# A graph layer on one core: block 0 from whole f32 inputs, gathers one step later, a reordered beginning

## The reference

```python
r = edge_vec / norm(edge_vec);  sh1 = sqrt(3) * r
s1 = concat(x[src][:, :8], x[dst][:, :8]);  v1 = the same of the vectors
w  = relu(emb @ fc1_w1 / sqrt(10)) @ fc1_w2 / 4          # 512 weights of an edge
s_t, v_t = sums over u of s1, v1 . sh1, s1 * sh1, v1 with w   # 8 scalars, 8 vectors
w2 = relu(emb @ fc2_w1 / sqrt(10)) @ fc2_w2 / 4          # 384 weights
scal, gates, vecs = the same kind of sums of s_t, v_t with w2
edge_out = concat(tanh(scal), vecs * tanh(gates)) * edge_weight
x = layernorm(x + segment_sum(edge_out, dst))
```

## Time and profile before

| | us |
|---|---|
| median of 3 runs | 746.08 (746.05 to 746.92) |
| the profiled execution | 744.64 |
| its span (first to last instruction) | 742.8 |
| PE busy | 687.2 (93%) |
| DVE busy | 691.7 (93%) |
| ACT busy | 560.2 (75%) |
| POOL busy | 528.0 (71%) |
| mean granted TensorE clock | 0.97 |

### The profile page before, as it was taken

One profiled execution on the slowest core, in us unless ns is written; L12 is line 12 of the kernel. 1 busy time (PEld: TensorE's weight loads), 2 busy tenths in 40 slices (PEclk: granted clock), 3 DMA queues, 4 the chain that ended last, 5 costly groups with the idle time before them and its releaser, 6 DMA issues.

```text
span 742.8 us, 19328 instructions
## 1 busy us (share of the span) xinstructions
PE 687.2 (93%) x5990; PEld 282.9 (38%) x5990; DVE 691.7 (93%) x1231; ACT 560.2 (75%) x1281; POOL 528.0 (71%) x653
## 2 busy tenths in 40 slices
PE   2359999999999999999999999999999999999984
PEld 2113334434443444344344444334434443444321
DVE  7488999999999999999999999999999999999986
ACT  3238887887888778888888888877788888878752
POOL 5676888778876887688768886787778876887200
PEclk7569999999999999999999999999999999999998
DMA  5412211111111211121112111211121111111000
GB/s 132 112 34 47 47 32 28 40 46 28 30 42 27 50 26 42 28 47 31 43 26 45 29 43 27 48 31 27 40 46 29 28 39 26 41 27 27 20 1 23
DMA packets 45822, 28.49 MB, mean 38 GB/s; under 512 B 23299, under 2 KB 43941, under 8 KB 45721
## 3 DMA queue, kind: packets, MB, share of 16 engines
q1 hardware_dynamic: 31402, 19.43, 9.9%
q0 software_dynamic: 13312, 6.84, 6.0%
q10 hardware_dynamic: 1006, 0.96, 0.5%
HBM read 22.46 MB, written 4.74 MB: 37 GB/s over the span
## 4 chain that ended last, share of the span: by engine, by line
PE 87%; DVE 4%; issue 2%; ACT 1%; POOL 1%; DVEq 0%; ACTq 0%
PE ps L1073 16%; PE ps L986 14%; PE ps L1004 13%; PE ps L993 9%; PE ps L1053 8%; PE ps L974 6%; PE ps L1029 5%; PE ps L1066 4%; PE ps L1060 3%; PE ps L964 3%; PE ps L1041 3%; PE ps L948 2%; PE ps L1021 2%; DVE p_s L751 2%; ACT v_s L528 1%
## 5 line engine op out<-in xcount | busy, mean ns | idle before, releaser
L374 POOL DMA_INDIRECT xs<-in_xp,src_i x416 | 401.0, 964 | 115.2 <-issue 104.3
L751 DVE TENSOR_TENSOR p_s<-ps,h 128x2048 f32<-128x2048 f32 x104 | 238.3, 2292 | 21.6 <-PE ps L1073 20.9
L791 DVE TENSOR_TENSOR z_s<-ps,h 128x2048 f32<-128x2048 f32 x104 | 237.6, 2284 | 1.3 <-PE ps L1029 1.2
L528 ACT CAST v_s<-ps 128x512 bf16<-128x512 f32 x312 | 182.2, 584 | 48.3 <-PE ps L986 43.2
L1073 PE MATMUL ps<-f,w_f 32*128 32x512 f32 x832 | 119.7, 642 | 4.3
L986 PE MATMUL ps<-p_s,sum_m 128*32 128x512 f32 x832 | 111.7, 605 | 0.6 <-DVE p_s L751 0.5
L1004 PE MATMUL ps<-z_s,w_z 128*32 128x512 f32 x832 | 110.8, 605 | 1.5 <-DVE z_s L791 1.5
L494 ACT COPY f<-ps 128x512 f32<-128x512 f32 x104 | 61.0, 587 | 41.9 <-PE ps L974 41.5
L993 PE MATMUL ps<-v_s,less 128*128 128x512 bf16 x208 | 81.1, 390 | 2.8 <-ACT v_s L528 2.6
L416 POOL TENSOR_TENSOR along<-fe,r 128x192 f32<-128x192 f32 x104 | 54.2, 521 | 32.8 <-ACT fe L506 26.3
L1053 PEld LDWEIGHTS ps<-ident,u 128*128 128x128 f32 x416 | 43.8, 141 | 87.6 <-issue 87.0
(11 more groups left out here) (129 smaller groups left out, 848.7 us busy)
## 6 DMA issues: line engine op xcount, KB each, us to landing
emb<-e_dram SPq DMA_DIRECT2D x309, 30.0 KB
xs<-in_xp,src_i POOLq DMA_INDIRECT x416
e_dram<-e_part SPq DMA_DIRECT2D x7, 360.0 KB, 3.0
e_in<-in_emb SPq DMA_DIRECT2D x8, 240.0 KB, 2.9
window<-x_dram SPq DMA_DIRECT2D x104, 7.9 KB
eo_all<-in_vec_t SPq DMA_DIRECT2D x1, 528.0 KB, 5.0
x_dram<-eo_all SPq DMA_DIRECT2D x1, 525.0 KB
place<-place_dram SPq DMA_DIRECT2D x26, 20.0 KB
```

The costliest lines, as they stand in the source:

```text
L374: nc.gpsimd.indirect_dma_start(xs_r[n][:, t, :], None, xp, bass.IndirectOffsetOnAxis(src_i[:, m * T + t:m * T + t + 1], axis=0)).then_inc( ...
L528: nc.scalar.copy(v_s[:], v_ps).then_inc(v_step, 1)
L751: nc.vector.tensor_tensor(p_s[:], ps[:, 0:4, :], h1_r[m % 2][:].unsqueeze(1).to_broadcast([128, 4, BE]), ALU.mult).then_inc(p_done, 1)
L791: nc.vector.tensor_tensor(z_s[:], ps[:, 0:4, :], h2_r[k % 3][:].unsqueeze(1).to_broadcast([128, 4, BE]), ALU.mult).then_inc(z_done, 1)
```

## The change

- The first block (WHOLE = 1) takes its MLP inputs and weights in f32, in whole, from the arguments (e_whole, w_whole), so its hidden layers need no parts; the buffers emb serve blocks 1 on.
- SP: bases and w2a are loaded earlier, the register loads for the first three windows are done ahead, windows 0 to 2 go out together, then the store of the first group of MLP inputs (which was in ScalarE's list), window 3, and the rest in another order. ScalarE's list loses the store, the wait for it and block 0's three loads; it gains the load of the rest of the vectors.
- POOL: clears the sums acc at the start (VectorE did), gathers blocks 0 and 1 whole before the steps, no longer makes the first group's remainders, and gathers block i + 4 in step i instead of i + 5.
- VectorE: constants that were made after the directions stand ahead of the first remainder of x; the first remainder of x stands ahead of the places; the first group's remainders are made here; the weights of the hidden layers are split in step -2, the repeat matrices made in step 0, the rest of the directions spread over steps -2 and 1 to 3; the sums are not cleared here.
- TensorE: hidden_1 of block 0 in step -3, two idle matmuls (keep_warm) at the end of step -2, waits for constants split accordingly.

```diff
+WHOLE = 1
...
+        e_whole = early(32 + HID, WHOLE * BE).rearrange("p (b e) -> p b e", b=WHOLE)
+        w_whole = early(32 + HID, 128)
...
-                base = sp.value_load(bases[0:1, m:m + 1], min_val=0, max_val=N - 1)
+                    base = sp.value_load(bases[0:1, m:m + 1], min_val=0, max_val=N - 1)
+                else:
+                    base = first_bases[m]
...
+            sp.dma_start(bases[:], bases_row).then_inc(bases_loaded, 16)
+            sp.dma_start(w2a_s, w2a).then_inc(w2a_loaded, 16)
+            for n in range(2):
+                sp.dma_start(e_whole[32 * n:32 * n + HID], emb[0:WHOLE * HID].rearrange("(b h) e -> h b e", h=HID)
+                             ).then_inc(whole_loaded, 16)
+                sp.dma_start(w_whole[32 * n:32 * n + HID], w1[0:HID, n, :]).then_inc(whole_loaded, 16)
             load_super(0)
-            sp.dma_start(w1_s, w1).then_inc(weights_loaded, 16)
-            sp.dma_start(w2a_s, w2a).then_inc(weights_loaded, 16)
-            sp.dma_start(bases[:], bases_row).then_inc(bases_loaded, 16)
+            sp.dma_start(w1_s, w1).then_inc(w1_loaded, 16)
...
+            sp.wait_ge(bases_loaded, 16)
+            first_bases = [sp.value_load(bases[0:1, m:m + 1], min_val=0, max_val=N - 1) for m in range(3)]
...
             load_window(1)
+            load_window(2)
+            store_super(0)
+            load_window(3)
             sp.wait_ge(emb_zeroed, 1)
-            load_window(2)
             load_emb(1)
-            sp.dma_start(vt[:, TA:TILES, :], vec_t[:, TA:TILES, :]).then_inc(vect_rest_loaded, 16)
-            load_window(3)
-            sp.dma_start(src_i[:, TA:TILES], src_t[:, TA:TILES]).then_inc(src_loaded, 16)
-            load_emb(2)
             sp.wait_ge(place_stored, 32)
             load_places(1)
-            sp.dma_start(w_z[:].rearrange("p n c -> p (n c)"), w2b).then_inc(weights_loaded, 16)
+            load_emb(2)
+            sp.dma_start(w_z[:].rearrange("p n c -> p (n c)"), w2b).then_inc(w2b_loaded, 16)
+            sp.dma_start(src_i[:, TA:TILES], src_t[:, TA:TILES]).then_inc(src_loaded, 16)
+            load_places(2)
             sp.dma_start(wgt_s[:], wgt).then_inc(wgt_loaded, 16)
             sp.dma_start(dst_i[:], dst_t).then_inc(dst_loaded, 16)
...
+            nc.gpsimd.memset(acc[:], 0.0).then_inc(acc_zeroed, 1)
             pool.wait_ge(src_loaded, 16)
-            gather(0, 0, 3)
-            rest_of_emb(0, 0)
-            gather(0, 3, T)
+            gather(0, 0, T)
+            gather(1, 0, T)
...
-                rest_of_emb(0, 1)
-                gather(1, 0, 2)
                 pool.wait_ge(r4_ready, 1)
                 for i in STEPS:
-                    if i < 1:
-                        if real(i + 3):
-                            directions(i + 3)
-                        if i == -3:
-                            gather(1, 2, T)
-
-                        if i == -3:
-                            gather(2, 0, T)
-                        if i == -2:
-                            gather(3, 0, 2)
-                        if i == -1:
-                            gather(3, 2, T)
-                        if i >= -1:
-                            gather(i + 5, 0, T)
-                    else:
-                        if real(i + 5):
-                            gather(i + 5, 0, 3)
-                        if real(i + 3):
-                            directions(i + 3)
-                        later_emb(i)
-                        if real(i + 5):
-                            gather(i + 5, 3, T)
+                    if real(i + 4) and i >= -1:
+                        gather(i + 4, 0, 3)
+                    if real(i + 3):
+                        directions(i + 3)
+                    if i == -2:
+                        gather(2, 0, T)
+                    later_emb(i)
+                    if real(i + 4) and i >= -1:
+                        gather(i + 4, 3, T)
...
+            act.dma_start(vt[:, TA:TILES, :], vec_t[:, TA:TILES, :]).then_inc(vect_rest_loaded, 16)
 
             act.wait_ge(warm_set, 1)
             nc.scalar.activation(warmed[:], warm[:], ACT.Sqrt)
             part_of_x(0)
             act.wait_ge(place_ready, 1)
             nc.scalar.copy(place_part[:, 0, :], place_f).then_inc(place_step, 1)
+            part_of_x(1)
             act.wait_ge(place_ready, 2)
             nc.scalar.copy(place_part[:, 1, :], place_sq).then_inc(place_step, 1)
-            part_of_x(1)
+            part_of_x(2)
             part_of_emb(0, 0)
-            part_of_x(2)
-            part_of_emb(0, 1)
             act.wait_ge(n2_ready, 1)
             nc.scalar.activation(nrm_t[:, 0:TA], n2_t[:, 0:TA], ACT.Sqrt).then_inc(norm_ready, 1)
-            act.wait_ge(e_part_ready, PARTS)
-            act.dma_start(e_dram[:, 0:SB * HID, :].rearrange("n r e -> r n e"), e_part[0:SB * HID]).then_inc(e_stored, 16)
             copy_oht(0)
-            act.wait_ge(emb_zeroed, 1)
-            act.wait_ge(e_stored, 16)
-            for first in (0, 32, 64):
-                act.dma_start(emb_r[0][first:first + PARTS * HID], e_dram[:, 0:HID, :]).then_inc(emb_loaded[0], 16)
...
-                if i == -1:
+                if i == 0:
                     act.wait_ge(n2_ready, 2)
                     nc.scalar.activation(nrm_t[:, TA:TILES], n2_t[:, TA:TILES], ACT.Sqrt).then_inc(norm_ready, 1)
-                if real(i + 3) and i < 2:
+                if real(i + 3) and i < -1:
                     copy_sources(i + 3)
+                if i == -3:
+                    part_of_emb(0, 1)
...
+                if real(i + 3) and -1 <= i < 2:
+                    copy_sources(i + 3)
...
+            link(nc.vector.tensor_copy(iota[:], iota_i[:]))
+            link(nc.vector.tensor_reduce(sel_w[:], ident[:].rearrange("p (j c) -> p c j", j=16), AX.X, ALU.add))
+            link(nc.vector.memset(sum_m[:, 3:4, :], 0.0))
+            nc.vector.tensor_copy(sum_m[:, 0:3, :], sel_w[:].unsqueeze(1).to_broadcast([128, 3, 8])).then_inc(consts_ready, 1)
+            link(nc.vector.tensor_reduce(of_group[:], ident[:].rearrange("p (g c) -> p g c", g=4), AX.X, ALU.add))
+            link(nc.vector.tensor_reduce(of_part[:], ident[:].rearrange("p (g n c) -> p n g c", g=4, n=4), AX.XY, ALU.add))
+            nc.vector.tensor_scalar(less[1][:], ident[:], of_part[:, 2:3], -1.0, ALU.mult, ALU.mult).then_inc(rep_step, 1)
+            link(nc.vector.tensor_tensor(of_part[:, 0:1], of_part[:, 0:1], of_part[:, 1:2], ALU.add))
+            link(nc.vector.tensor_tensor(of_part[:, 1:2], of_part[:, 1:2], of_part[:, 2:3], ALU.add))
+            link(nc.vector.tensor_tensor(of_part[:, 0:1], of_part[:, 0:1], of_part[:, 2:3], ALU.add))
+            nc.vector.tensor_scalar(less[0][:], ident[:], of_part[:, 1:2], -1.0, ALU.mult, ALU.mult).then_inc(rep_step, 1)
+
+            rest_of_x(0)
             dve.wait_ge(dst_rows_loaded, 32)
             link(nc.vector.tensor_copy(base_f[:], base_i[:]))
             link(nc.vector.tensor_copy(place_f, dst_row_i))
             link(nc.vector.tensor_scalar(place_f, place_f, base_f[:], None, ALU.subtract))
             nc.vector.engine_nop().then_inc(place_ready, 1)
             nc.vector.tensor_tensor(place_sq, place_f, place_f, ALU.mult).then_inc(place_ready, 1)
-            rest_of_x(0)
-            link(nc.vector.tensor_scalar(bad, place_f, float(WIN), None, ALU.is_ge))
+            dve.wait_ge(x_rest_ready, 1)
+            rest_of_x(1)
...
+            rest_of_emb(0)
+            directions(0, TA, TILES).then_inc(r4_step, 1)
+            rest_of_emb(1)
+
+            def repeat_constants():
+                for g in range(4):
+                    link(nc.vector.tensor_scalar(sel_g[:, g, :], sel_w[:], of_group[:, g:g + 1], of_part[:, 0:1], ALU.mult, ALU.mult))
+                    nc.vector.tensor_copy(rep_m[:, g], sel_g[:, g, :].unsqueeze(1).to_broadcast([128, 16, 8])).then_inc(rep_step, 1)
...
-                nc.vector.tensor_copy(dst_f[:], dst_i[:]).then_inc(place_ready, 1)
-                nc.vector.memset(acc[:], 0.0).then_inc(acc_zeroed, 1)
...
+                if i == 0:
+                    repeat_constants()
                 if real(i + 2):
                     sum_along(i + 2)
+                if i == -2:
+                    first_weights()
                 if i == 0:
+                    second_weights()
+                if i == 2:
                     late_constants()
 
-                for step, at_step in enumerate((-2, -2, 0, 0, 0, 1, 1, 1)):
+                for step, at_step in ((1, -2), (2, 1), (3, 2), (4, 2), (5, 2), (6, 2), (7, 3)):
...
+                if m < WHOLE:
+                    pe.wait_ge(whole_loaded, 64)
+                    nc.tensor.matmul(h1_ps, w_whole[0:HID], e_whole[0:HID, m, :], start=True, stop=True).then_inc(h1_done, 1)
+                    return
+                if m == WHOLE:
+                    pe.wait_ge(weights_ready, 3)
+                pe.wait_ge(emb_loaded[m % 3], 48 * ((m - WHOLE) // 3 + 1))
...
```

(4 more changed lines are left out.)

81 lines of the change are left out of this document (40 added, 41 removed).

## The result

| | before | after |
|---|---|---|
| median, us | 746.07 | 764.16 (759.3 to 766.1, 4 runs) |
| ratio | | 1.0233, 95% interval 1.0206 to 1.026 |
| profiled execution / its span, us | 744.64 / 742.8 | 764.14 / 762.3 |
| product of block 0 starts at | 37.64 | 30.56 |
| product of block 4 | 70.30 | 59.97 |

A forecast was written before the change was run, and what follows sets the result against it. TensorE was taken to bound the kernel, with VectorE about 3% to spare. The ramp's gain of 8.85 us (7.8 + 0.6 + 0.45) less 7.6 us for late gathers gave -1.25 us: 744.8 us, range 738.0 to 751.0.

The forecast's parts named there:

- Part 1: The front up to product 0: it starts at 29.8 instead of 37.64, a gain of 7.8 us, bounds 5.6 to 9.6.
- the lock: At the start, POOL's clearing of the sums holds up VectorE's constants: 2.4 us, bounds 0 and 2.9.
- Part 2: From product 0 to product 4: 32.0 us against 32.66, a gain of 0.6, bounds 3.2 to -1.3.
- Part 3: Steady part: gathers one step later make TensorE lose 0.95 us in each of eight groups, 7.6 us, bounds 4.8 and 9.
- The slack: In a group's steps, ScalarE's third part of v is ready 1.05 us before TensorE's repeat needs it, after the hand-over.
- The landing: In the groups, a gather is usable 1.3 to 1.8 us after its issue ends, so block 20's copy is late.
- The feedback: In a group's second step, POOL's remainder slips by 0.15 us because the copy of block 19 is late too.
- C: Rival, slower: gathers land late in each group, at 2.3 us costing 12.8 in all, so 750.0 us; chance 0.23.
- A: The ramp's gain and the groups' loss nearly cancel: 741.5 to 748 us; chance 0.43.
- B: Rival, faster: the late gathers don't reach TensorE, groups lose 0.2 us each, so 738.8 us; chance 0.23.
- D: Rival, slower: the front doesn't shorten, the ramp gains 4 us instead of 8.85, so 749.7 us; chance 0.09.
- E: Rival: block 0 still hangs on the stored inputs, the ramp gains only 1 to 2 us, so 752 us; chance 0.02.

The follow-up runs named there:

- The third experiment: The changed kernel, but from step 2 on ScalarE copies the third part of v before it copies the sources: 736.4 us, ratio 0.9863.

## Why the prediction was wrong

**Part 1, right.** Product 0 was put at 29.8 and came at 30.56. The timeline of all engines in the changed kernel, step by step:

```profile
2.37 3.56 DVE L678 CAST rank<-rank_i 5x126 f32<-5x126 int32 x1
...
3.09 2.77 POOL L441 MEMSET acc<- 128x3200 f32 x1
...
16.89 0.76 SPq L336 DMA_DIRECT2D x_dram<-eo_all  x2
...
21.41 1.47 SPq L285 DMA_DIRECT2D window<-x_dram  x3
...
23.51 0.29 PE L1059 MATMUL ps<-window,oht 126*128 126x32 bf16 x4 [0.21 <-DMA window<-x_dram]
...
26.08 1.09 PE L990 MATMUL ps<-ident,fe 128*128 128x128 f32 x4
...
28.41 2.07 PE L1101 MATMUL ps<-f,w_f 32*128 32x512 f32 x8
...
30.56 2.29 DVE L761 TENSOR_TENSOR p_s<-ps,h 128x2048 f32<-128x2048 f32 x1 [1.13 <-PE ps L1101]
```

The cast that takes 0.85 us in the earlier trace rows now takes 3.56 and ends at 5.93, 0.07 after POOL's memset: the lock was there, at 2.77 us of memset where 2.8 to 3.0 was taken, and with the clearing moved the cast is back at 0.86. The x store is at 16.89 (16.7 predicted), the windows at 21.41 (21.0), the transposition at 26.08 (25.5). One link was read the other way: rows 0 waited for the window's landing, not for ScalarE's MLP input, at nearly the same time.

**Part 2, right in sign, short in size.** 29.41 us instead of 32.0, just beyond the bound of 29.5. VectorE's work was 25.96 us (26.5 predicted), its wait for POOL's directions 2.1 (2.0). The third term, hand-overs and low clock, was put at 3.5 and is the 1.35 us that are left; this is the one that was mis-sized. The clock was 0.94 over the stretch, where 0.82 had been carried over from before.

**The first group.** It was to give back 0.45 us in the ramp. It cost 2.1: the same mechanism as in the other seven groups works here already.

**Part 3, the step that failed.** The place, the engines, the eight groups and the unharmed plain steps were as predicted. The price of a group was 2.1 to 5.2 us instead of 0.6 to 1.1, 28.1 us in all instead of 7.6. Four terms:

- *The slack.* "1.1 us of slack, 1.05 after the hand-over" was measured to the repeat at 164.25, as if it were the first reader of the third part of v. The transposition of u stands before it and waits for the same part. In the kernel before, TensorE's timeline has it here:

```profile
163.24 0.64 PE L1053 MATMUL ps<-ident,u 128*128 128x128 f32 x4
```

  The cast of the earlier trace rows ends at 163.14, 0.10 us before, and those 0.10 us are the hand-over itself: in the changed kernel, where TensorE stands waiting, it is 0.09. So there was no slack in such a step. This is the error that mattered most: with 0 in the place of 1.05, the prediction's own sum gives 2.0 a group, 16.0 us, and 753.2 us, slower and outside its range.
- *The landing.* 1.3 to 1.8 us was read off blocks 1 and 2. In the groups, between the end of the last issue and the copy, it was 1.5 to 2.8 us, nine of the 16 at 2.0 or more. The Trainium skill's figure of about 2.0 us (DMA: Bandwidth & Descriptors, Anatomy of one DMA), which the prediction had set aside for its rows, was nearer than the rows; 2.7 and 2.8, second landings of two groups, are beyond it too, and why was not tried.
- *The feedback.* The remainder was to slip by 0.15 us. It slipped by its 1.10 of waiting: TensorE, 1.51 late in the first step, hands ScalarE its inputs later, so ScalarE's part of the MLP input (151.69) is later, so POOL's second remainder waits for it at 152.38, and the fourth gather behind it is later again. The third experiment shows this loop from the other side, since that second remainder no longer waits when TensorE isn't late.
- *The clock.* Behind gaps of 2.41, 2.30 and 1.68 us it fell to half, for 1.15 us more in each of three groups. No term had this.

"Plain steps cost nothing" held. The late copies were to be three a group; of the 19 waits in the whole trace three are in the ramp, so it was two a group.

**The rivals.** C named the right mechanism and sign and put 0.23 on it; its rule, landing less 0.7, gives 1.3 and 2.1 us for landings of 2.0 and 2.8, and the two steps of this group cost 1.6 and 3.6 (1.15 of it the clock). It had the same wrong slack, and counted one late landing a group where there were two that add up. A, the forecast, and B fell with the slack. D fell: the front did shorten, by 7.1 us; E with it, since block 0 didn't hang on the stored inputs. The last steps' 1.7 us were in nobody's sum.

## What to carry to other kernels

Before you price a late instruction, list every wait on its semaphore in the consumer's code, those that guard a shared PSUM bank included, and take the slack to the first of them in that engine's order; the data's reader may be the second. Where a queue both issues DMAs and waits for another engine, issue first (here worth about 28 us, by one moved line), and on the engine that receives, put what the critical engine needs ahead of what may land late. A stall that delays the engine on which its own cause depends is no single term: sum it over the loop, and count the clock behind a gap.

## What the runs showed of the hardware

- After a gap of 1.51 us TensorE went on at a granted 1.00 (2.4 GHz). After one of 2.41 it did so for some 0.9 us more and then fell to the 1.2 GHz level: eight matmuls took 1.94 us instead of 1.06, and that step's mean was 0.83. The length of the gap alone doesn't decide it: in the kernel before with late gathers the clock fell behind one gap of 1.85 us and not behind another of 1.85, and in the changed kernel behind one of 1.68. Where it fell, the step was 1.15 us longer.
- The same code ran at either level: from product 0 to product 1 it took 6.74 us at 1.00 in the changed kernel and 8.29 at 0.54 in the one with the idle matmuls, which differ only in later steps.
- A POOL memset of 128x3200 f32, 2.77 us, held a VectorE cast of 5x126 to 3.56 us, though the cast had begun at 2.37 and that memset only at 3.09. Behind the short memset of line 428 alone it takes 0.85, and a cast of the same size 0.21 alone.
- Gathers of four tiles that were waited for landed 1.5 to 2.8 us after the end of their last issue in the groups of the changed kernel, against 1.3 and 1.8 in the beginning of the one before.
